# First four K tiles loaded from one tensor of W beside X, the first over two queues; VectorE rounds the first W; 18 warm-up products

## The reference

```python
w = jnp.einsum('bpf,mf->bpm', features, W_ft) + b_ft      # (1024, 2, 5128) x (512, 5128)
accumulator = stm * w
l1_x = jnp.clip(accumulator, 0.0, 1.0).reshape(features.shape[0], -1)
l2_x = jnp.clip(l1_x @ W1.T + b1, 0.0, 1.0)               # W1 is (32, 1024)
return l2_x @ W2.T + b2                                   # W2 is (1, 32)
```

## Time and profile before

| | before |
|---|---|
| time of the kernel, median of 3 runs | 397.88 us (397.74 to 398.15) |
| span of the profiled execution (first to last instruction) | 396.4 us |
| time outside the span, as median minus span | 1.5 us |
| PE busy | 392.8 us, 99% of the span |
| DVE, ACT busy | 346.9 us, 197.6 us |

### The profile page before, as it was taken

One profiled execution on the slowest core, in us unless ns is written; L12 is line 12 of the kernel. 1 busy time (PEld: TensorE's weight loads), 2 busy tenths in 40 slices (PEclk: granted clock), 3 DMA queues, 4 the chain that ended last, 5 costly groups with the idle time before them and its releaser, 6 DMA issues.

```text
span 396.4 us, 4869 instructions
## 1 busy us (share of the span) xinstructions
PE 392.8 (99%) x1862; PEld 323.7 (82%) x1862; DVE 346.9 (88%) x347; ACT 197.6 (50%) x207; POOL 14.7 (4%) x34
## 2 busy tenths in 40 slices
PE   8999999999999999999999999999999999999997
PEld 6888888888888888888888888888788888878886
DVE  3999999999999999999997789999787754999624
ACT  5565556633484434444334864344433447863500
POOL 0000034041000000000000000000000000000000
PEclk9999999999999999999999999999999999999999
DMA  8999979989976677666607689887667778774000
GB/s 271 394 398 400 383 247 362 342 256 230 327 255 233 237 254 263 243 220 235 233 0 256 225 317 397 327 308 236 203 233 257 241 217 247 245 246 132 0 2 3
DMA packets 30775, 97.85 MB, mean 247 GB/s; under 512 B 4024, under 2 KB 10176, under 8 KB 25312
## 3 DMA queue, kind: packets, MB, share of 16 engines
q1 hardware_dynamic: 29392, 95.18, 69.0%
q0 software_dynamic: 1072, 2.10, 1.7%
q10 hardware_dynamic: 288, 0.26, 0.2%
HBM read 96.87 MB, written 0.00 MB: 244 GB/s over the span
## 4 chain that ended last, share of the span: by engine, by line
PE 99%; DVE 0%; issue 0%; DVEq 0%
PE sums L595 94%; PE sums L672 3%; PE sums L711 1%; PE sums L698 1%; PE sums L688 0%; PE sums L706 0%; DVE res L528 0%; DVE hid L522 0%; DVE idle L531 0%; DVEq L527 0%
## 5 line engine op out<-in xcount | busy, mean ns | idle before, releaser
L595 PE MATMUL sums<-x_hi,w_hi 128*128 128x512 f32 x544 | 167.2, 391 | 0.0
L595 PE MATMUL sums<-x_hi,w_lo 128*128 128x512 f32 x544 | 166.5, 389 | 0.0
L595 PEld LDWEIGHTS sums<-x_hi,w_hi 128*128 128x128 f32 x544 | 102.1, 188 | 21.9 <-issue 0.7
L595 PEld LDWEIGHTS sums<-x_hi,w_lo 128*128 128x128 f32 x544 | 102.4, 188 | 21.3
L595 PE MATMUL sums<-x_lo_home,w_hi 128*128 128x512 f32 x384 | 118.4, 389 | 0.0
L355 ACT ACTIVATE x_hi<-xs 128x2048 fp32r<-128x2048 f32 x58 | 110.7, 1908 | 2.2 <-DVE xs L490 1.8
L350 ACT ACTIVATE w_hi<-ws 128x512 fp32r<-128x512 f32 x58 | 36.9, 636 | 147.1 <-PE sums L595 139.0
L499 DVE TENSOR_TENSOR x_lo_home<-xs,x_hi 128x2048 fp32r<-128x2048 f32 x40 | 91.3, 2283 | 12.3 <-ACT x_hi L355 12.3
L595 PEld LDWEIGHTS sums<-x_lo_home,w_hi 128*128 128x128 f32 x384 | 72.1, 188 | 15.0
L483 DVE TENSOR_TENSOR xs<-xs 128x2048 f32<-128x2048 f32 x20 | 45.6, 2281 | 0.7 <-DMA xs<-x_p 0.7
L496 DVE TENSOR_TENSOR w_lo<-ws,w_hi 128x512 fp32r<-128x512 f32 x58 | 39.6, 683 | 6.2 <-ACT w_hi L350 6.1
(11 more groups left out here) (72 smaller groups left out, 199.5 us busy)
## 6 DMA issues: line engine op xcount, KB each, us to landing
xs<-x_p SPq DMA_DIRECT2D x40, 1024.0 KB, 5.7
xs<-x_p SPq DMA_DIRECT2D x56, 512.0 KB, 6.4
ws<-w_p SPq DMA_DIRECT2D x56, 256.0 KB, 3.5
ws<-w_p SPq DMA_DIRECT2D x44, 128.0 KB, 4.7
open_x<-x_p SPq DMA_DIRECT2D x3, 512.0 KB, 6.2
xr_raw<-x_rest POOLq DMA_DIRECT2D x1, 1024.0 KB, 8.5
stm_all<-stm SPq DMA_DIRECT2D x1, 1024.0 KB, 7.6
open_x<-x_p SPq DMA_DIRECT2D x2, 256.0 KB, 4.3
```

The source lines that it names most:

```text
L595: return nc.tensor.matmul(sums[:, bank, :], w[:, m * P:(m + 1) * P], x[:, c * BANK:(c + 1) * BANK], start=start, stop=stop, skip_group_che ...
```

## The change

The host lays out a further input `o_p`, 128 rows of 5120 numbers: for each of the first four steps the 256 columns of W and behind them the 1024 columns of X. It is loaded into one buffer `open_all`, which takes the place of `open_x` and `open_w`. The first piece (256 columns of W, 512 of X: 384 KB) is two loads, rows 0 to 63 issued by SP and rows 64 to 127 by ScalarE. The second piece is one load with the rest of X of step 0 and W of step 1 (384 KB), the third X of step 1; W and X of steps 2 and 3 come in one load each. The first W is rounded by VectorE, not by ScalarE. There are 18 warm-up products, not 22.

```diff
-WARM_UP = 22
+WARM_UP = 18
...
-        open_x = sb("open_x", [P, STAGED, COLS], at=c_at)
+        open_all = sb("open_all", [P, STAGED * (MH + COLS)], at=c_at)
...
-        open_w = sb("open_w", [P, STAGED, MH], at=xr_at)
...
-        open_w_loaded = [sem(f"open_w_loaded{j}") for j in range(STAGED)]
-        open_x_loaded = [sem(f"open_x_loaded{j}") for j in range(STAGED + 1)]
+        open_first = sem("open_first")
+        open_x0b_w1 = sem("open_x0b_w1")
+        open_loaded = [sem(f"open_loaded{j}") for j in range(STAGED)]
+        w0_hi = sem("w0_hi")
...
+        def open_at(g):
+            return g * (MH + COLS)
+
+        def open_w(g):
+            return open_all[:, open_at(g):open_at(g) + MH]
+
+        def open_x(g):
+            return open_all[:, open_at(g) + MH:open_at(g + 1)]
+
+        def load_first(engine, lo, hi):
+            engine.dma_start(open_all[lo:hi, 0:MH + BANK], o_p[lo:hi, 0:MH + BANK]).then_inc(open_first, 16)
...
-            sp.dma_start(open_x[:, 0, 0:BANK], x_p[0, :, 0, 0:BANK]).then_inc(open_x_loaded[0], 16)
-            sp.dma_start(open_x[:, 0, BANK:COLS], x_p[0, :, 0, BANK:COLS]).then_inc(open_x_loaded[STAGED], 16)
+            load_first(sp, 0, P // 2)
+            sp.dma_start(open_all[:, MH + BANK:open_at(1) + MH], o_p[:, MH + BANK:open_at(1) + MH])\
+                .then_inc(open_x0b_w1, 16)
             for g, pos in OPEN_HALVES[1:2 * STAGED]:
                 if pos == 0:
-                    if g > 1:
-                        sp.dma_start(open_w[:, g, :], w_p[g, :, 0, :]).then_inc(open_w_loaded[g], 16)
-                    sp.dma_start(open_x[:, g, :], x_p[g, :, 0, :]).then_inc(open_x_loaded[g], 16)
+                    a = open_at(g) + (MH if g == 1 else 0)
+                    sp.dma_start(open_all[:, a:open_at(g + 1)], o_p[:, a:open_at(g + 1)]).then_inc(open_loaded[g], 16)
...
-                if pos == 0 and g < STAGED:
-                    sc.wait_ge(open_w_loaded[g], 16)
-                    nc.scalar.activation(w_hi[:, g % HI, 0, :], open_w[:, g, :], ACT.Copy).then_inc(open_hi, 1)
-                    sc.wait_ge(open_x_loaded[g], 16)
-                    for i, (a, b) in enumerate(pieces(g, 0)):
+                if (g, pos) == (0, 0):
+                    sc.wait_ge(open_first, 16 * 2)
+                    for i, (a, b) in enumerate(pieces(0, 0)):
                         if i:
-                            sc.wait_ge(open_x_loaded[STAGED], 16)
-                        nc.scalar.activation(x_hi[:, g % HI, 0, a:b], open_x[:, g, a:b], ACT.Copy).then_inc(open_hi, 1)
+                            sc.wait_ge(open_x0b_w1, 16)
+                        nc.scalar.activation(x_hi[:, 0, 0, a:b], open_x(0)[:, a:b], ACT.Copy).then_inc(open_hi, 1)
...
-            for g in range(2):
-                sc.dma_start(open_w[:, g, :], w_p[g, :, 0, :]).then_inc(open_w_loaded[g], 16)
+            load_first(sc, P // 2, P)
...
+            dve.wait_ge(open_first, 16 * 2)
+            nc.vector.tensor_copy(w_hi[:, 0, 0, :], open_w(0)).then_inc(w0_hi, 1)
...
                 for i, cs in enumerate(groups):
-                    pe.wait_ge(open_hi, before + 2 + i)
+                    if n == 0:
+                        pe.wait_ge(w0_hi, 1)
+                    pe.wait_ge(open_hi, hi + 2 + i)
...
+    o_p = np.concatenate([part for g in range(STAGED) for part in (w_p[g, :, 0], x_p[g, :, 0])], axis=1)
     laid_out = {
+        "o_p": np.ascontiguousarray(o_p),
```

More of the change, by code:

```diff
@@ L53, in pass_of, with feature_net @@
     return f, g - f * K_PAIRS
-def feature_net(nc, x_p, w_p, x_rest, w_rest, stm, b_ft, w1_t, b1, w2_t, b2, out):
+def feature_net(nc, o_p, x_p, w_p, x_rest, w_rest, stm, b_ft, w1_t, b1, w2_t, b2, out):
     L1 = w1_t.shape[2]
@@ L107, in feature_net @@
         wr_low = sb("wr_low", [P, 2, MH], F32R, at=c_at + 8 * COLS)
-        xr_at = place[0]
         xr = sb("xr", [P, 2, COLS], F32R)
-        open_w = sb("open_w", [P, STAGED, MH], at=xr_at)
         wr = sb("wr", [P, 2, MH], F32R)
@@ L227, in pieces, with lo_before, hi_before @@
             return ((0, COLS),)
-        def halves_before(n):
+        def lo_before(n):
             return sum(1 + len(pieces(*half)) for half in OPEN_HALVES[:n])
+        def hi_before(n):
+            return lo_before(n) - 1
+        def open_at(g):
[6 more added lines that the diff above has]
+            engine.dma_start(open_all[lo:hi, 0:MH + BANK], o_p[lo:hi, 0:MH + BANK]).then_inc(open_first, 16)
         def x_sums(g):
@@ L317, in open_half @@
                     sc.wait_ge(step_done if pos else a_done, g - HI + 1)
-                if pos == 0 and g < STAGED:
-                    sc.wait_ge(open_w_loaded[g], 16)
-                    nc.scalar.activation(w_hi[:, g % HI, 0, :], open_w[:, g, :], ACT.Copy).then_inc(open_hi, 1)
-                    sc.wait_ge(open_x_loaded[g], 16)
-                    for i, (a, b) in enumerate(pieces(g, 0)):
-                        if i:
-                            sc.wait_ge(open_x_loaded[STAGED], 16)
-                        nc.scalar.activation(x_hi[:, g % HI, 0, a:b], open_x[:, g, a:b], ACT.Copy).then_inc(open_hi, 1)
+                if (g, pos) == (0, 0):
+                    sc.wait_ge(open_first, 16 * 2)
+                    for i, (a, b) in enumerate(pieces(0, 0)):
+                        if i:
+                            sc.wait_ge(open_x0b_w1, 16)
+                        nc.scalar.activation(x_hi[:, 0, 0, a:b], open_x(0)[:, a:b], ACT.Copy).then_inc(open_hi, 1)
+                elif pos == 0 and g < STAGED:
+                    if g > 1:
+                        sc.wait_ge(open_loaded[g], 16)
+                    nc.scalar.activation(w_hi[:, g % HI, 0, :], open_w(g), ACT.Copy).then_inc(open_hi, 1)
+                    sc.wait_ge(open_loaded[g], 16)
+                    for a, b in pieces(g, 0):
+                        nc.scalar.activation(x_hi[:, g % HI, 0, a:b], open_x(g)[:, a:b], ACT.Copy).then_inc(open_hi, 1)
                 elif pos == 0:
@@ L432, in open_low @@
             def open_low(n, g, pos):
-                before = halves_before(n)
+                before = hi_before(n)
                 if pos == 0 and g < STAGED:
-                    w_src, x_src = open_w[:, g, :], open_x[:, g, :]
+                    w_src, x_src = open_w(g), open_x(g)
                 elif pos == 0:
@@ L439, in open_low @@
                     w_src, x_src = ws[:, raw_w(g) + 1, :], xs[:, TST + g, :]
-                dve.wait_ge(open_hi, before + 1)
+                if n == 0:
+                    dve.wait_ge(w0_hi, 1)
+                else:
+                    dve.wait_ge(open_hi, before + 1)
                 nc.vector.tensor_tensor(w_lo[:, slot(g), pos, :], w_src, w_hi[:, g % HI, pos, :].bitcast(F32),
@@ L454, in sums_of @@
                 if f == 0:
-                    if staged:
-                        dve.wait_ge(open_w_loaded[g], 16)
+                    if g == 0:
+                        dve.wait_ge(open_first, 16 * 2)
+                    if staged and g < 2:
+                        dve.wait_ge(open_x0b_w1, 16)
+                    if staged and g > 0:
+                        dve.wait_ge(open_loaded[g], 16)
                     dve.wait_ge(s_loaded[n], t_count(k))
@@ L460, in sums_of @@
                     dve.wait_ge(t_loaded[n], t_count(k))
[L461 to L465, removed]
+                    if not staged:
                         dve.wait_ge(x_loaded[n], x_count(g))
-                    b11 = open_x[:, g, :] if staged else xs[:, j, :]
+                    b11 = open_x(g) if staged else xs[:, j, :]
                     for a, b in pieces(g, 1):
@@ L602, in open_products @@
             def open_products(n, g, pos):
-                before = halves_before(n)
+                hi, lo = hi_before(n), lo_before(n)
                 _, _, bank = HALVES[0][pos]
@@ L612, in open_products @@
                             product(bank + m * 2 + c, wh, xh, m, c, g == 0)
-                    pe.wait_ge(open_lo, before + 1)
+                    pe.wait_ge(open_lo, lo + 1)
                     for m in range(2):
@@ L616, in open_products @@
                             product(bank + m * 2 + c, wl, xh, m, c, False)
-                    pe.wait_ge(open_lo, before + 2 + i)
+                    pe.wait_ge(open_lo, lo + 2 + i)
                     for c in cs:
```

## The result

Over ten runs each, the changed kernel takes 399.08 us (398.61 to 399.86) and the one before 398.05 us (397.74 to 398.93): ratio 1.0023, 95% interval 1.0013 to 1.0033. It is slower by about 1.0 us. The time lies outside the forecast range (397.0 to 398.6), on the side of the second rival.

What follows compares the result with a forecast made beforehand. PE, with a matmul in flight for 99% of the span, was taken as the bound, leaving only its opening to win. Span 396.4 - 0.31 = 396.1 us plus 1.5 us outside it gave 397.6 us, range 397.0 to 398.6.

Steps and rivals of the forecast that it cites:

- the second rival: PE's opening: the pause between warm-up and first product keeps the clock low until 11.14 us; 399.6 us, chance 0.13.
- What bounds the kernel: Whole kernel: PE is busy 99% of the span, so only the start and speed of its first real products can gain.
- Rounding on VectorE: Opening: VectorE's copy of the first W takes 0.42 us, hidden beside ScalarE's 0.61 us, and costs nothing.
- The first load: Opening: the first 384 KB, split in two, land at 4.3 us instead of 4.8, at worst no gain.
- The first rival: Opening load: the split brings nothing, landing stays at 4.8 us, gain 0.06; 397.8 us, chance 0.20.
- What the start is worth: PE's opening: the clock rises at about 7.05 us either way, so 0.62 us of earlier start gains 0.31 us.
- Start of the first product: PE's opening: the first real product starts at 5.15 instead of 5.77 us, after a pause of about 0.28 us.
- What could take it back: Later loads: X of step 1 still lands at 7.1 us, leaving 0.39 us to spare, so the gain passes through.
- The third rival: PE's opening: the clock rises before the first product, so the whole 0.62 us counts; 397.3 us, chance 0.12.
- The sum: Whole kernel: a gain of 0.31 us, to 396.1 us of span and a median of 397.6 us.

Runs made afterwards that it cites:

- the version by columns: Changed kernel, 18 warm-up products, first piece split into W on ScalarE's queue and X on SP's, 128 rows each: 397.25 us, ratio 0.9983 to the kernel before.

## Why the prediction was wrong

*What bounds the kernel.* Right. What the change altered lies in the opening, in when PE's real products start, when X of step 1 comes, and at which clock. One figure beside it was off without harm to the sum: every run that is listed with its span has 1.7 to 2.0 us outside it, not 1.5, so the span of 396.4 belongs to an execution of about 398.2 us and not to the median.

*Rounding on VectorE.* Right: 0.29 us against the bound of 0.42, hidden under ScalarE's 0.63.

*The first load.* This is the step that failed first. The prediction gave it a landing of 4.3, bounded by "no gain at all, 4.8"; it landed at 5.3. The bound excluded a loss without a reason: it counted bytes and took for granted that a load of 64 rows is issued like one of 128. It took 0.56 us instead of 0.41 and landed later than before. The first rival, with 4.8, was nearer; its time of 397.8 us was not right, since it too took the old landing as the worst. Behind it stands a rule of the Trainium skill ("DMA: Bandwidth & Descriptors", section "Rules for kernel authors"): not two transfers to disjoint partition halves, but one transfer of 128 partitions. The runs agree with that advice: the one load was there at 4.25 and 4.56, the two halves at 4.71 to 5.53.

*What the start is worth.* This step failed too. "The clock rises at about 7.05 in either case, if the pause doesn't matter" took the rise of one trace for a fixed place, and the factor of one half, 0.31 us for 0.62, hangs on it. With at most a short pause ahead of it (0.3 us) the rise came anywhere from 4.05 to about 7.05 in the traces, and with a pause of 1 us or more ahead of it at 9.2 and later.

*Start of the first product.* The chain of it was right (rounding 0.63, then the weight load, product at about +0.2); with 5.33 in place of 4.3 it gives 6.1 to 6.2, and 6.13 was seen. The pause became 1.0 to 1.3 us instead of 0.28.

*What could take it back.* The landing of X of step 1 at 7.1 failed with the same step: the loads on SP's queue moved with the slow issues. (The bytes ahead of it are 768 KB; the 1280 KB of the prediction include X of step 1 itself, before and after alike.) It was rounded from 8.14, and PE, with 0.39 us to spare in the forecast, waited for it (9.26, had 8.90).

*The rivals.* The second, given 0.13, is what happened in part of the executions: the pause lets the clock rise late. Shown by the three traces in which the clock had not risen when a pause of 1 us or more began (rises at about 9.2, 9.5 and 10, later than in any other trace), by 18 against 14 and 10 warm-up products (1.0023, 1.0038, 1.0049; the last two not told apart), and by 22, which take the loss away at unchanged loads. Its size was off: I had the rise 5.99 us after the first product, at 11.1, and in each run. It was not the change's 18 products alone: with the first piece at 4.15 or 4.25 they leave no such pause and cost nothing, with the loads of before or the late ones they cost 0.2%. The argument against it, that PE works on both sides of the pause, was no argument. The third rival, given 0.12, is what the version by columns shows in its trace: an early rise lets the whole 0.7 us of the earlier start count.

*The sum.* -0.31 us was forecast, +1.0 measured. In the two traces of the change the spans are 396.8 and 397.8 against 396.4. In the first the late loads cost 0.4 although the clock was high from the first real product on, where the trace of before lost 0.6 us to the low clock; in the second it is 1.4, with the late rise on top. The median's +1.0 lies between. Two parts make it up. With 22 warm-up products the late loads cost nothing against before, and some 0.14% against the same kernel with the loads of before. Four products fewer cost 0.2% more with these loads, as they do with the loads of before; with an early first piece they cost nothing that can be told. So had the first piece landed at 4.3, the shorter warm-up would have done no harm. With the first piece by columns the start moves as the forecast had it, and the median gains about 0.7 us, more than the 0.31 forecast. In its one trace 0.7 us are the start and 0.4 the clock's earlier rise; how these are shared in the other runs is not shown.

## What to carry to other kernels

Here the warm-up has to reach to the first real work, in late executions too: with an early first load four products more made no measurable difference (0.9986 against 0.9983), while with the late loads, and with those of before, four too few cost 0.2%. Before a load is split, look at how its form is issued: here two loads of 128 rows that share out the columns were as good as one, and two of 64 rows delayed themselves and what was queued behind them. And a rise of the clock that is read from one trace is one sample, not a fixed time. A lower bound on a gain (at worst nothing) needs a reason like any other.

## What the runs showed of the hardware

The time to issue a load differed with its rows: 0.41 us for 128 rows of 3 KB, 0.55 to 0.58 for 64 rows of 3 KB, and 0.82 for a load of 128 rows behind them with the other queue busy too.

The clock rises at no fixed time. While PE worked from 1.06 us on with no pause above some 0.2 us, the distance of starts halved at about 4.05 us (before with 18 products, first trace), 4.4 (the change), 5.5 (by columns), 6.1 (one load, 18 products) and 7.0 (before, and one load with 22). The earliest of them, from narrow windows of that trace, with starts 0.13 and 0.11 us apart, where 256 columns had taken 0.21:

```profile
4.02 0.52 PE L711 MATMUL sums<-idle 128*128 128x256 bf16 x3
4.15 0.49 PE L711 MATMUL sums<-idle 128*128 128x256 bf16 x3
4.26 0.38 PE L711 MATMUL sums<-idle 128*128 128x256 bf16 x2
```

A cause of spread lies far from the opening: in the trace of the kernel with old loads and rounding on VectorE (a run of 398.80 us) PE waits near 224 us. From its chain of waits:

```profile
207.66 7.16 DMA xs<-x_p
...
214.84 1.24 DVE xs L513
...
216.10 1.93 ACT x_hi L375
...
223.67 0.58 ACT c_late L402
...
224.39 54.86 PE sums L620 x240
```

One load of X there took 7.16 us to land (5.3 for the same load in the trace of before), and by way of VectorE and ScalarE it delayed the emptying of the banks that PE waited for: two products start 1.20 us apart where 0.23 is usual. The trace with 22 warm-up products and late loads has the same wait (7.03 us to land; its next product after 223.90 starts at 224.96), the other eleven traces have none. So one trace of a kernel can differ by most of a microsecond from another for a reason far from the opening; how often it happens in the runs without a trace is not known, nor why the load is late.
